# A sandwich layer whose FFN blocks compute the first matmul of two tiles by Strassen's scheme

## The chip, the cores and the metric

The kernel runs on one core of a Trainium2 chip. The metric is the device time of one execution in microseconds (us), lower is better. Engines are named as in the profile: PE (TensorE, matmuls), PEld (its weight loads), DVE (VectorE), ACT (ScalarE), POOL (GpSimd), SP (SyncE, which issues DMAs). Each engine runs its own instructions strictly in the order in which the program lists them; engines wait for each other only through semaphores.

## The reference, cut to what matters

2048 tokens of 256 features, in fp32: a gated linear attention with a layernorm on each side, and then six FFN blocks, again with a layernorm ahead and behind.

```
def _block(x, w1, b1, w2, b2):                     # HIDDEN = 1024, DIM = 256
    h = jax.nn.gelu(jnp.einsum('bsd,hd->bsh', x, w1) + b1, approximate=False)
    return jnp.einsum('bsh,dh->bsd', h, w2) + b2 + x
for i in range(6):
    x = _block(x, W1[i], B1[i], W2[i], B2[i])
    if i < 5:
        x = _layernorm(x, LN_G[i], LN_B[i])
```

The change touches the FFN blocks 1 to 4 alone. The attention, block 0 and block 5 compute what they did.

## The kernel before, in words

**Tiles.** The tokens are cut into four tiles of 512 (`TOK`). In the FFN, tile t of block b has the number n = 4b + t. Features lie on the partitions: a tile's input is two chunks (k = 0, 1) of 128 features by 512 tokens. Every fp32 operand X is kept as a rounded high part and a rest (`XH` and `XL` for the input, `WH` and `WL` for weights, `HH` and `HL` for the hidden layer), and a product is three matmuls, low by high, high by low, high by high, accumulated in fp32 in PSUM.

**One unit.** The hidden layer's 1024 features are eight slices j. For each (n, j), `mm1` (L326) makes 2 chunks x 3 = 6 matmuls of 512 columns into one of the four PSUM banks 0 to 3. ACT reads the bank twice, `ghi` (L970, gelu into `HH`) and `gf` (L979, gelu in place). DVE's `hlo` (L564) subtracts the two and writes `HL`. Then `mm2` (L340) makes 6 more matmuls into the tile's two accumulators (banks 4 to 7). `HH` and `HL` are rings of four slices. The PE list of blocks 1 to 5 is a loop over g = 8n + j (L400): `mm1` of unit g, then `mm2` of unit g - 3 (`LAG`).

**Between the blocks.** When the eighth `mm2` of a tile is done, DVE adds bias and residual (`y`, L572). Then comes a layernorm over features, that is over partitions, in many steps: `sum1` (POOL), `tr1`, `red1` (DVE), `put1` and `got1` (DMAs through DRAM, which spread the sums over the partitions), `tot1`, `mub`, `ctr` (DVE), `sqr` (ACT), `sum2` (POOL), `tr2`, `red2` (DVE), `put2`, `got2` (DMAs), `tot2`, `vae` (DVE), `rsd` (POOL, L1259, a power of -1/2), `rsb`, `nn` (DVE). At last `xhi` (ACT) and `xlo` (DVE) make the two parts of the next block's input, on which `mm1` of tile n + 4 waits. `got1` and `got2` (L1347 and L1359) are four transfers each, one for each 32 partitions.

**Weights.** A block's weights come in four pieces of 128x1024 (`ldp` on SP, into the two halves of `STG`); ACT's `wp_hi` and POOL's `wp_lo`, two halves of 512 each, split a piece.

**Order.** Every engine's list is written out by hand up to about tile 5 and for the last tiles; between them loops over n give each tile the same order on DVE, ACT, POOL and SP.

## Time and profile before

| | |
|---|---|
| median of 3 runs | 625.25 us (625.02 to 625.41) |
| the profiled execution's own time | 625.31 us |
| its span in the profile | 623.5 us (1.8 us lie around it) |
| PE busy | 617.3 us, 99% of the span, 2893 matmuls |
| DVE busy | 459.9 us, 74% |
| ACT busy | 409.0 us, 66% |
| POOL busy | 248.7 us, 40% |
| granted TensorE clock | 0.998 of full speed (2.4 GHz) |

Busy times of engines are not to be added, since they run side by side. A matmul's duration in the profile is the time from its start to its modelled end, and matmuls overlap; the distance between the starts of two is what one costs. An engine's idle time is put down to what released it.

### The profile page before, as it was taken

Reading aid. Unit: us, or ns where it says so; the run is one execution under the profiler, and the core shown is the slowest. Engines: PE = TensorE matmul, PEld = TensorE weight load, DVE = VectorE, ACT = ScalarE, POOL = GpSimd, SP = SyncE. Lnnn points to the kernel's source line nnn. Section 1 sums busy time; section 2 is a strip of 40 time slices with the busy share of each in tenths; the row PEclk is TensorE's granted clock in tenths of the full one; section 3 lists DMA queues with packets and bytes.
Section 4 is the critical chain, followed back from the end, with each engine's and each line's share of the span. In section 5 each row is a group of like instructions: output and inputs, shape, how many; then the busy total and the mean of one; then the engine's idle time right before and its main releaser. Section 6 shows DMA issues by size and latency. Waiting matters only on the chain.

```text
span 623.5 us, 8868 instructions
## 1 busy us (share of the span) xinstructions
PE 617.3 (99%) x2893; PEld 516.5 (83%) x2893; DVE 459.9 (74%) x826; ACT 409.0 (66%) x688; POOL 248.7 (40%) x233
## 2 busy tenths in 40 slices
PE   9999999999999999999999999999999999999996
PEld 7888888888888888888888888888888888888886
DVE  6999758886677778676787667767766867666676
ACT  6999986778756675566566556755656665555554
POOL 6666501537434353334532253442344422301234
PEclk9999999999999999999999999999999999999999
DMA  7210000003111020101200110200111100003544
GB/s 293 69 35 1 2 2 0 4 1 106 36 39 40 7 68 6 37 6 37 58 20 3 39 39 2 72 6 5 37 39 38 38 4 6 5 3 68 94 91 156
DMA packets 55821, 25.13 MB, mean 40 GB/s; under 512 B 46816, under 2 KB 51808, under 8 KB 55776
## 3 DMA queue, kind: packets, MB, share of 16 engines
q1 hardware_dynamic: 53376, 24.05, 15.2%
q10 hardware_dynamic: 2400, 0.52, 0.4%
q8 instruction: 23, 0.38, 0.3%
q14 instruction: 22, 0.18, 0.1%
HBM read 20.03 MB, written 4.52 MB: 39 GB/s over the span
## 4 chain that ended last, share of the span: by engine, by line
PE 95%; DVE 1%; DMA 1%; POOL 1%; ACT 0%; issue 0%; ACTq 0%; SPq 0%
PE BK L166 47%; PE BK L356 40%; PE BK L306 4%; PE BK L267 1%; PE BK L270 1%; PE BK L268 1%; PE BK L240 1%; PE BK L260 0%; PE BK L252 0%; PE BK L251 0%; DMA X<-in_x 0%; PE BK L230 0%; DVE R L709 0%; DMA turns<-TB 0%; DMA R<-turns 0%; DVE ST L675 0%
## 5 line engine op out<-in xcount | busy, mean ns | idle before, releaser
L976 ACT ACTIVATE HH<-BK,SM 128x512 fp32r<-128x512 f32 x192 | 132.1, 689 | 153.3 <-PE BK L166 148.3
L569 DVE TENSOR_TENSOR HL<-BK,HH 128x512 fp32r<-128x512 f32 x192 | 131.2, 685 | 84.0 <-ACT BK L982 82.0
L166 PE MATMUL BK<-XH,WL 128*128 128x512 f32 x416 | 162.4, 390 | 0.0
L166 PE MATMUL BK<-XL,WH 128*128 128x512 f32 x416 | 162.1, 390 | 0.0
L166 PE MATMUL BK<-XH,WH 128*128 128x512 f32 x416 | 162.0, 389 | 0.0
L356 PE MATMUL BK<-HH,WL 128*128 128x512 f32 x368 | 143.5, 390 | 0.0
L356 PE MATMUL BK<-HH,WH 128*128 128x512 f32 x368 | 143.2, 389 | 0.0
L356 PE MATMUL BK<-HL,WH 128*128 128x512 f32 x368 | 143.2, 389 | 0.0
L982 ACT ACTIVATE BK<-BK,SM 128x512 f32<-128x512 f32 x192 | 125.2, 655 | 0.0
L166 PEld LDWEIGHTS BK<-XH,WL 128*128 128x128 f32 x416 | 78.1, 188 | 16.6 <-DVE MS L551 0.3
L166 PEld LDWEIGHTS BK<-XH,WH 128*128 128x128 f32 x416 | 78.1, 188 | 16.3
L166 PEld LDWEIGHTS BK<-XL,WH 128*128 128x128 f32 x416 | 78.1, 188 | 15.8
L1263 POOL TENSOR_TENSOR RN<-VN,MH 128x16 f32<-128x16 f32 x20 | 58.7, 2935 | 62.4 <-DVE VN L628 62.4
L356 PEld LDWEIGHTS BK<-HL,WH 128*128 128x128 f32 x368 | 69.1, 188 | 14.3
L356 PEld LDWEIGHTS BK<-HH,WH 128*128 128x128 f32 x368 | 69.1, 188 | 14.3
L356 PEld LDWEIGHTS BK<-HH,WL 128*128 128x128 f32 x368 | 69.1, 188 | 14.2
L1177 POOL TENSOR_TENSOR WL<-STG,WH 128x512 fp32r<-128x512 f32 x48 | 64.5, 1361 | 36.7 <-ACT WH L850 36.6
L1257 POOL TENSOR_TENSOR SA<-SA,TB 128x512 f32<-128x512 f32 x20 | 25.9, 1293 | 127.3 <-ACT TB L991 127.3
L1253 POOL TENSOR_TENSOR SA<-R 128x512 f32<-128x512 f32 x20 | 25.9, 1293 | 39.6 <-DVE R L577 39.6
L1001 ACT ACTIVATE XH<-R,SM 128x512 fp32r<-128x512 f32 x40 | 27.7, 724 | 19.6 <-DVE R L642 19.6
L577 DVE SCALAR_TENSOR_TENSOR R<-BK,SM,R 128x512 f32<-128x512 f32 x46 | 33.5, 731 | 3.4 <-PE BK L356 3.4
L642 DVE SCALAR_TENSOR_TENSOR R<-R,SM,MB 128x512 f32<-128x512 f32 x40 | 35.5, 922 | 0.5
(165 smaller groups left out, 790.1 us busy)
## 6 DMA issues: line engine op xcount, KB each, us to landing
STG<-in_w SPq DMA_DIRECT2D x24, 512.0 KB, 3.8
G<-sums SPq DMA_DIRECT2D x160, 8.0 KB, 1.7
out<-R SPq DMA_DIRECT2D x16, 128.0 KB, 2.0
X<-in_x SPq DMA_DIRECT2D x3, 512.0 KB, 7.7
R<-turns SPq DMA_DIRECT2D x3, 512.0 KB, 4.1
turns<-SA SPq DMA_DIRECT2D x12, 64.0 KB, 2.0
sums<-P SPq DMA_DIRECT2D x40, 8.0 KB, 1.4
R<-in_wv SPq DMA_DIRECT2D x1, 512.0 KB, 5.4
```

Of the source, the lines that this page charges most:

```text
L166: r = eng.matmul(dst, s, m, start=i == 0, stop=i == len(todo) - 1)
L356: r = eng.matmul(acc_of(n)[k][:, :], w, h[:, hs, :], start=(j == 0 and i == 0), stop=(j == 7 and i == 2))
L569: eng.tensor_tensor(HL[:, g % HR, :], bank["mm1", n, j][:, :], HH[:, g % HR, :].bitcast(f32), ALU.subtract).then_inc(S["hlo"], 1)
L577: eng.scalar_tensor_tensor(feat(t, k), by_chunk(acc_of(n)[k][:, :]), BS[:, 2 * b + k:2 * b + k + 1], feat(t, k), ALU.add, ALU.add).then_in ...
L642: eng.scalar_tensor_tensor(feat(t, k), feat(t, k), LG[:, 2 * b + k:2 * b + k + 1], by_chunk(MB[:, 1, :]), ALU.mult, ALU.mult).then_inc(S[" ...
L976: eng.activation(HH[:, g % HR, :], bank["mm1", n, j][:, :], ACT.Gelu, bias=B1[:, 8 * (n // 4) + j:8 * (n // 4) + j + 1]).then_inc(S["ghi"], 1)
L982: eng.activation(ps[:, :], ps[:, :], ACT.Gelu, bias=B1[:, 8 * (n // 4) + j:8 * (n // 4) + j + 1]).then_inc(S["gf"], 1)
L1001: eng.activation(by_chunk(XH[:, F_SLOT[t], k, :]), feat(t, k), ACT.Identity, bias=LB[:, 2 * b + k:2 * b + k + 1]).then_inc(S["xhi"], 1)
L1177: eng.tensor_tensor(WL[:, b % 2, a:a + 512], STG[:, p % 2, 512 * h:512 * h + 512], WH[:, b % 2, a:a + 512].bitcast(f32), ALU.subtract).the ...
L1253: eng.tensor_tensor(by_chunk(SA[:, :]), feat(n % 4, 0), feat(n % 4, 1), ALU.add).then_inc(S["sum1"], 1)
L1257: eng.tensor_tensor(SA[:, :], SA[:, :], TB[:, :], ALU.add).then_inc(S["sum2"], 1)
L1263: eng.tensor_tensor(RN[:, :], VN[:, :], MH[:, :], ALU.pow).then_inc(S["rsd"], 1)
```

## The change

In blocks 1 to 4 the tiles 0 and 1 become a **pair**. Their first layer is a product of 2x2 blocks: the weights (two halves of the hidden features by two chunks, for each q of 0 to 3 the slices q and q + 4) and the input (two chunks by two tiles). Instead of eight block products of three matmuls each, seven are made, `prod1` to `prod7`, on sums of blocks:

- Sums of weights, `sadd` on POOL from `STG` into `SB` (four of 128x512 a pair), split by `shi` (ACT, two of 128x1024, into `UH` and `OH`, which the attention had used) and `slo` (POOL, four of 128x512, into `UL` and `OL`).
- Sums of inputs, `tsum` on DVE into `QB` (four a pair), split by `thi` (ACT) and `tlo` (DVE). Of the four plain inputs three are still needed and split, `bhi` (ACT) and `blo` (DVE).
- Products that go into more than one result are carried by copies: for each q ACT's `bcopy` copies bank a to bank c, and `tcopy` copies bank e to `KB`; DVE's `dsum` writes c + `KB` to bank d, and `esum` writes c + `KB` to bank e. PE goes on accumulating on a, c and d.

The four units of a q are numbered by `place`: (second tile, q), (first tile, q), (first, q + 4), (second, q + 4). Their `ghi`, `gf`, `hlo` and `mm2` stay what they were; in the PE list one `mm2` stands behind every two products. Behind the pair the last three `mm2` come right after the first `mm1` of tile 2.

Also: `put1` and `put2` write the sums to DRAM in another arrangement, from which `got1` and `got2` fetch them in **one** transfer of 128 rows of 256 bytes. All lists of blocks 1 to 4 (and the end of block 0's, from the place where DVE has its last `l2_mv`) are written out anew, for DVE, ACT, POOL and SP. PE's list up to the end of block 0 is what it was, and so are all lists of the last tiles.

```
+def place(n, j):
+    if not paired(n):
+        return 8 * n + j
+    return 32 * (n // 4) + 4 * (j % 4) + ((1, 2) if n % 4 == 0 else (0, 3))[j // 4]
...
+            def product(dst, s, m, first, last):
+                for i, (w, v) in enumerate(((s[1], m[0]), (s[0], m[1]), (s[0], m[0]))):
+                    r = eng.matmul(dst[:, :], w, v, start=first and i == 0, stop=last and i == 2, skip_group_check=True)
+                return r
+
+            def prod1(b, q, a, c, d, e):
+                claim(a)
+                pe.wait_ge(S["plo"], 7 * (b - 1) + 3)
+                pe.wait_ge(S["wp_lo"], 8 * b + 4)
+                bank["pair", b, q] = BK[a], BK[c], BK[d], BK[e]
+                bank["before", b, q] = freed[c], freed[d], freed[e]
+                for x, (n, j) in ((a, (4 * b + 1, q)), (d, (4 * b, q)), (e, (4 * b, q + 4)), (c, (4 * b + 1, q + 4))):
+                    bank["mm1", n, j] = BK[x]
+                    freed[x] = S["hlo"], place(n, j) + 1
+                product(BK[a], w_ffn(b, 128 * q, 128), home(B11), True, True).then_inc(S["prod"], 1)
+
+            def prod2(b, q):
+                pe.wait_ge(S["plo"], 7 * (b - 1) + 6)
+                pe.wait_ge(S["pcopy"], 8 * (b - 1) + 2 * q + 1)
+                product(bank["pair", b, q][0], w_ffn(b, 1024 + 128 * q, 128), home(B21), False, True).then_inc(S["mm1"], 1)
+
+            def prod3(b, q):
+                pe.wait_ge(S["plo"], 7 * (b - 1) + 1)
+                pe.wait_ge(S["slo"], 4 * b)
+                pe.wait_ge(S["padd"], 8 * (b - 1) + 2 * q + 1)
+                product(bank["pair", b, q][2], s_weights(3, q), home(B22), False, True).then_inc(S["mm1"], 1)
+
+            def prod4(b, q):
+                pe.wait_ge(S["plo"], 7 * b)
+                pe.wait_ge(S["padd"], 8 * (b - 1) + 2 * q + 2)
+                product(bank["pair", b, q][1], w_ffn(b, 1536 + 128 * q, 128), t_home(b, 3), False, True).then_inc(S["mm1"], 1)
+
+            def prod5(b, q):
+                before = bank["before", b, q][2]
+                pe.wait_ge(*before)
+                pe.wait_ge(S["plo"], 7 * (b - 1) + 4)
+                pe.wait_ge(S["slo"], 4 * b - 3)
+                product(bank["pair", b, q][3], s_weights(0, q), t_home(b, 1), True, True).then_inc(S["prod"], 1)
+
+            def prod6(b, q):
+                pe.wait_ge(S["plo"], 7 * (b - 1) + 5)
+                pe.wait_ge(S["slo"], 4 * b - 2)
+                pe.wait_ge(S["pcopy"], 8 * (b - 1) + 2 * q + 1)
+                product(bank["pair", b, q][1], s_weights(1, q), t_home(b, 2), False, True).then_inc(S["prod"], 1)
+
+            def prod7(b, q):
+                pe.wait_ge(S["plo"], 7 * (b - 1) + 2)
+                pe.wait_ge(S["slo"], 4 * b - 1)
+                pe.wait_ge(S["padd"], 8 * (b - 1) + 2 * q + 1)
+                product(bank["pair", b, q][1], s_weights(2, q), t_home(b, 0), False, True).then_inc(S["mm1"], 1)
...
-            for g in range(8 * 4, 8 * (4 * NB - 1)):
-                mm1(g // 8, g % 8, STEADY[g % 4])
-                mm2((g - LAG) // 8, (g - LAG) % 8)
+            for b in range(1, NB):
+                if b in PAIRED:
+                    a, e, c, d = STEADY
+                    for q in range(4):
+                        g = 32 * b + 4 * q
+                        mm2(*unit(g - 3))
+                        prod1(b, q, a, c, d, e)
+                        prod5(b, q)
+                        mm2(*unit(g - 2))
+                        prod2(b, q)
+                        prod6(b, q)
+                        mm2(*unit(g - 1))
+                        prod3(b, q)
+                        prod7(b, q)
+                        mm2(*unit(g))
+                        prod4(b, q)
+                        e, c, d = d, e, c
+                first_g = 32 * b + (16 if b in PAIRED else 0)
+                for g in range(first_g, min(32 * b + 32, 8 * (4 * NB - 1))):
+                    mm1(*unit(g), STEADY[g % 4])
+                    if b not in PAIRED or g > first_g + 2:
+                        mm2(*unit(g - LAG))
+                    elif g == first_g:
+                        for back in (3, 2, 1):
+                            mm2(*unit(g - back))
...
+            def tsum(b, i):
...
+                ve.wait_ge(S["nn"], 2 * n + (2, 3, 3, 4)[i])
+                if i > 1:
+                    ve.wait_ge(S["tsum"], 4 * (b - 1) + i)
+                dst, bias = by_chunk(QB[:, i, :]), LB[:, p + 1:p + 2]
+                if i == 0:
+                    ve.wait_ge(S["bias"], 2)
+                    r = eng.scalar_tensor_tensor(dst, feat(0, 1), DL[:, b - 1:b], feat(0, 0), ALU.add, ALU.subtract)
+                elif i == 1:
+                    r = eng.tensor_tensor(dst, feat(0, 0), feat(1, 0), ALU.subtract)
+                elif i == 2:
+                    r = eng.scalar_tensor_tensor(dst, feat(0, 1), bias, by_chunk(QB[:, 1, :]), ALU.add, ALU.subtract)
+                else:
+                    r = eng.scalar_tensor_tensor(dst, feat(1, 1), bias, by_chunk(QB[:, 2, :]), ALU.add, ALU.subtract)
+                r.then_inc(S["tsum"], 1)
+            def blo(b, i):
+                t, k = ((0, 1), (1, 0), (1, 1))[i]
+                hi, lo = b_home(i)
+                ve.wait_ge(S["phi"], 7 * (b - 1) + (1, 3, 6)[i])
+                eng.scalar_tensor_tensor(by_chunk(lo), feat(t, k), LB[:, 2 * (b - 1) + k:2 * (b - 1) + k + 1],
+                                         by_chunk(hi.bitcast(f32)), ALU.add, ALU.subtract).then_inc(S["plo"], 1)
+
+            def tlo(b, i):
+                hi, lo = t_home(b, i)
+                ve.wait_ge(S["phi"], 7 * (b - 1) + (2, 4, 5, 7)[i])
+                eng.tensor_tensor(lo, QB[:, i, :], hi.bitcast(f32), ALU.subtract).then_inc(S["plo"], 1)
+
+            def dsum(b, q):
+                _, c, d, _ = bank["pair", b, q]
+                ve.wait_ge(S["prod"], 12 * (b - 1) + 3 * q + 3)
+                ve.wait_ge(S["pcopy"], 8 * (b - 1) + 2 * q + 2)
+                ve.wait_ge(*bank["before", b, q][1])
+                eng.tensor_tensor(d[:, :], c[:, :], KB[:, q % 2, :], ALU.add).then_inc(S["padd"], 1)
+
+            def esum(b, q):
+                _, c, _, e = bank["pair", b, q]
+                ve.wait_ge(S["mm1"], place(4 * b, q + 4) + 1)
+                ve.wait_ge(S["pcopy"], 8 * (b - 1) + 2 * q + 2)
+                eng.tensor_tensor(e[:, :], c[:, :], KB[:, q % 2, :], ALU.add).then_inc(S["padd"], 1)
...
+
+            def bhi(b, i):
...
+                eng.activation(by_chunk(b_home(i)[0]), feat(t, k), ACT.Identity,
+                               bias=LB[:, 2 * (b - 1) + k:2 * (b - 1) + k + 1]).then_inc(S["phi"], 1)
+
+            def thi(b, i):
...
+                eng.activation(t_home(b, i)[0], QB[:, i, :], ACT.Copy).then_inc(S["phi"], 1)
+
+            def shi(b, h):
...
+                eng.activation((UH, OH)[h][:, :, :], SB[:, 2 * h:2 * h + 2, :], ACT.Copy).then_inc(S["shi"], 1)
+
+            def bcopy(b, q):
+                a, c, _, _ = bank["pair", b, q]
+                ac.wait_ge(S["prod"], 12 * (b - 1) + 3 * q + 1)
+                ac.wait_ge(*bank["before", b, q][0])
+                eng.activation(c[:, :], a[:, :], ACT.Copy).then_inc(S["pcopy"], 1)
+
+            def tcopy(b, q):
...
+                eng.activation(KB[:, q % 2, :], bank["pair", b, q][3][:, :], ACT.Copy).then_inc(S["pcopy"], 1)
+
+            def sadd(b, i):
...
+                a11, a21 = STG[:, 1, 0:512], STG[:, 1, 512:1024]
+                a12, a22 = STG[:, 0, 0:512], STG[:, 0, 512:1024]
+                if i in (1, 3):
+                    po.wait_ge(S["sadd"], 4 * (b - 1) + (1 if i == 1 else 2))
+                left, right, op = ((a21, a22, ALU.add), (SB[:, 0, :], a11, ALU.subtract), (a11, a21, ALU.subtract),
+                                   (a12, SB[:, 1, :], ALU.subtract))[i]
+                eng.tensor_tensor(SB[:, i, :], left, right, op).then_inc(S["sadd"], 1)
+
+            def slo(b, i):
+                hi, lo = (UH, OH)[i // 2], (UL, OL)[i // 2]
+                po.wait_ge(S["shi"], 2 * (b - 1) + i // 2 + 1)
+                eng.tensor_tensor(lo[:, i % 2, :], SB[:, i, :], hi[:, i % 2, :].bitcast(f32),
+                                  ALU.subtract).then_inc(S["slo"], 1)
...
             def ldp(p):
                 b, i = (p - 1) // 4, (p - 1) % 4
                 if p == 2:
-                    sp.wait_ge(S["wo_lo"], 1)
+                    sp.wait_ge(S["w_lo"], W_LO["o"])
                 elif p > 2:
                     sp.wait_ge(S["wp_lo"], 2 * (p - 2))
+                if b in PAIRED and i > 1:
+                    sp.wait_ge(S["sadd"], 4 * (b - 1) + i + 1)
                 src = (w1 if i < 2 else w2)[b][:, (i % 2) * 1024:(i % 2) * 1024 + 1024]
                 eng.dma_start(STG[:, p % 2, :], src).then_inc(S["ldp1"] if p % 2 else S["ldp0"], 16)
 
             def put1(n):
                 sp.wait_ge(S["red1"], n + 1)
-                eng.dma_start(SUMS[n, 0], P1[:, n % 2, :]).then_inc(S["put1"], 16)
+                eng.dma_start(SUMS[n, 0].rearrange("q (g b) -> g q b", g=4), P1[:, n % 2, :]).then_inc(S["put1"], 16)
 
             def got1(n):
                 sp.wait_ge(S["put1"], 16 * n + 16)
-                if n:
-                    sp.wait_ge(S["tot1"], n)
-                for h in range(4):
-                    eng.dma_start(G1[32 * h:32 * h + 32, n % 2],
-                                  SUMS[n, 0].rearrange("(g q) b -> q g b", g=4)).then_inc(S["got1"], 16)
+                if n > 1:
+                    sp.wait_ge(S["tot1"], n - 1)
+                eng.dma_start(G1[:, n % 2].rearrange("p g b -> p (g b)"),
+                              SUMS[n, 0].unsqueeze(0).to_broadcast([4, 32, 64])).then_inc(S[f"got1_{n % 2}"], 16)
```

**PE, block 2, first q of the pair.** Bank 2 is c, bank 0 is d, banks 4 to 7 accumulate `mm2`. The changed list, from `prod6` to `prod3`:

```order
L403 MATMUL BK2<-XH,UL 128x512
L403 MATMUL BK2<-XL,UH 128x512
L403 MATMUL BK2<-XH,UH 128x512
L471 MATMUL BK4<-HH,WL 128x512
L471 MATMUL BK4<-HH,WH 128x512
L471 MATMUL BK4<-HL,WH 128x512
L471 MATMUL BK5<-HH,WL 128x512
L471 MATMUL BK5<-HH,WH 128x512
L471 MATMUL BK5<-HL,WH 128x512
L403 MATMUL BK0<-XH,OL 128x512
L403 MATMUL BK0<-XL,OH 128x512
L403 MATMUL BK0<-XH,OH 128x512
```

The same place in the list before, from the second half of `mm1` (8, 2) over `mm2` (7, 7):

```order
L166 MATMUL BK1<-XH,WL 128x512
L166 MATMUL BK1<-XL,WH 128x512
L166 MATMUL BK1<-XH,WH 128x512
L356 MATMUL BK4<-HH,WL 128x512
L356 MATMUL BK4<-HH,WH 128x512
L356 MATMUL BK4<-HL,WH 128x512
L356 MATMUL BK5<-HH,WL 128x512
L356 MATMUL BK5<-HH,WH 128x512
L356 MATMUL BK5<-HL,WH 128x512
L166 MATMUL BK2<-XH,WL 128x512
L166 MATMUL BK2<-XL,WH 128x512
L166 MATMUL BK2<-XH,WH 128x512
```

Six matmuls of one `mm1` became two products of three on different banks, one of which (on bank 0) waits for DVE's `dsum`, and only one `mm2` of six lies ahead of it.

**DVE, the same pair, from the second `esum` to the third `dsum`.** L830 is `dsum`, L836 `esum`, L706 `hlo`; the others are steps of the layernorms of tiles 6 and 7:

```order
L836 TENSOR_TENSOR BK0<-BK1,KB 128x512
L721 STREAM_TRANSPOSE TB<-SA 128x512
L706 TENSOR_TENSOR HL<-BK2,HH 128x512
L725 TENSOR_REDUCE P1<-TB 128x16
L706 TENSOR_TENSOR HL<-BK0,HH 128x512
L759 TENSOR_REDUCE VS<-G2 128x16
L765 TENSOR_SCALAR VN<-VS 128x16
L706 TENSOR_TENSOR HL<-BK1,HH 128x512
L731 TENSOR_REDUCE MU<-G1 128x16
L771 STREAM_TRANSPOSE MB<-RN 128x512
L737 STREAM_TRANSPOSE MB<-MU 128x512
L830 TENSOR_TENSOR BK1<-BK0,KB 128x512
```

A piece of the list before, between the same kinds of steps (L569 is `hlo`, L577 `y`):

```order
L569 TENSOR_TENSOR HL<-BK1,HH 128x512
L569 TENSOR_TENSOR HL<-BK2,HH 128x512
L612 STREAM_TRANSPOSE TB<-SA 128x512
L577 SCALAR_TENSOR_TENSOR R<-BK6,SM,R 128x4x128
L616 TENSOR_REDUCE P2<-TB 128x16
L577 SCALAR_TENSOR_TENSOR R<-BK7,SM,R 128x4x128
L569 TENSOR_TENSOR HL<-BK0,HH 128x512
L584 STREAM_TRANSPOSE TB<-SA 128x512
L588 TENSOR_REDUCE P1<-TB 128x16
L569 TENSOR_TENSOR HL<-BK3,HH 128x512
```

Two additions on which PE waits now stand in the row, between the steps of two layernorms, where before `hlo` and one tile's layernorm (with the next tile's first steps) alternated.

**DVE, ahead of the same pair**, the stretch in which its inputs are made (L804 to L810 `tsum`, L817 `blo`, L823 `tlo`, L771 `rsb`, L779 `nn`, L721 `tr1`):

```order
L817 SCALAR_TENSOR_TENSOR XL<-R,SM,XH 128x512
L779 SCALAR_TENSOR_TENSOR R<-R,SM,MB 128x4x128
L706 TENSOR_TENSOR HL<-BK1,HH 128x512
L806 TENSOR_TENSOR QB<-R 128x512
L779 SCALAR_TENSOR_TENSOR R<-R,SM,MB 128x4x128
L808 SCALAR_TENSOR_TENSOR QB<-R,SM,QB 128x512
L706 TENSOR_TENSOR HL<-BK2,HH 128x512
L810 SCALAR_TENSOR_TENSOR QB<-R,SM,QB 128x512
L823 TENSOR_TENSOR XL<-QB,XH 128x512
L817 SCALAR_TENSOR_TENSOR XL<-R,SM,XH 128x512
L823 TENSOR_TENSOR XL<-QB,XH 128x512 x2
L817 SCALAR_TENSOR_TENSOR XL<-R,SM,XH 128x512
```

Before, the end of tile 5's layernorm stood at this place, between `hlo` of (7, 5) and the tile's end (L634 is `rsb`, L642 `nn`, L648 `xlo`, L594 `tot1`):

```order
L569 TENSOR_TENSOR HL<-BK1,HH 128x512
L569 TENSOR_TENSOR HL<-BK2,HH 128x512
L634 STREAM_TRANSPOSE MB<-RN 128x512
L642 SCALAR_TENSOR_TENSOR R<-R,SM,MB 128x4x128 x2
L569 TENSOR_TENSOR HL<-BK0,HH 128x512
L648 SCALAR_TENSOR_TENSOR XL<-R,SM,XH 128x512 x2
L594 TENSOR_REDUCE MU<-G1 128x16
```

Before, two `nn` and two `xlo` stood in each tile's stretch. Now 13 instructions that make the pair's inputs (two `nn`, four `tsum`, three `blo`, four `tlo`) stand in the last four units ahead of the pair, between `hlo` of (7, 3) and of (7, 7).

## Rows read from the trace of the kernel before

**Rows 1.** Page: span, busy time and count of each engine, chain by engine and line:

```profile
span 623.5 us, 8868 instructions
PE 617.3 (99%) x2893; PEld 516.5 (83%) x2893; DVE 459.9 (74%) x826; ACT 409.0 (66%) x688; POOL 248.7 (40%) x233
PE 95%; DVE 1%; DMA 1%; POOL 1%; ACT 0%; issue 0%; ACTq 0%; SPq 0%
```

**Rows 2.** A stretch as long as a block: us, PE, PEld, DVE, ACT, POOL busy (count), clock:

```profile
300.04:387.08 87.04, 87.04 (x385) 72.10 (x385) 63.40 (x101) 53.11 (x85) 32.99 (x20) 1.00 0.12 29
```

**Rows 3.** Timeline, one unit: start, duration (us), engine, line; idle and releaser bracketed:

```profile
302.13 0.39 PE L166 MATMUL BK<-XH,WH 128*128 128x512 f32 x1
302.13 0.19 PEld L356 LDWEIGHTS BK<-HH,WL 128*128 128x128 f32 x1
302.36 0.39 PE L356 MATMUL BK<-HH,WL 128*128 128x512 f32 x1
302.56 0.69 ACT L976 ACTIVATE HH<-BK,SM 128x512 fp32r<-128x512 f32 x1 [1.48 <-PE BK L166]
303.14 0.66 ACT L982 ACTIVATE BK<-BK,SM 128x512 f32<-128x512 f32 x1
305.86 0.66 ACT L982 ACTIVATE BK<-BK,SM 128x512 f32<-128x512 f32 x1
306.55 0.69 DVE L569 TENSOR_TENSOR HL<-BK,HH 128x512 fp32r<-128x512 f32 x1 [0.63 <-ACT BK L982]
```

**Rows 4.** Groups by line and form: busy us, mean ns; idle before, releaser:

```profile
L976 ACT ACTIVATE HH<-BK,SM 128x512 fp32r<-128x512 f32 x192 | 132.1, 689 | 153.3 <-PE BK L166 148.3 <-PE BK L356 3.4 <-PE BK L371 1.0
L569 DVE TENSOR_TENSOR HL<-BK,HH 128x512 fp32r<-128x512 f32 x192 | 131.2, 685 | 84.0 <-ACT BK L982 82.0 <-PE BK L356 1.5 <-issue 0.3
L521 DVE SCALAR_TENSOR_TENSOR BK<-KB,BK 128x512 f32<-128x512 f32 x8 | 5.5, 691 | 2.0 <-ACT KB L942 1.3 <-PE BK L166 0.7
L961 ACT ACTIVATE OH<-QB 128x512 fp32r<-128x512 f32 x16 | 10.1, 628 | 0.7 <-DVE QB L533 0.7
L850 ACT ACTIVATE WH<-STG 128x1024 fp32r<-128x1024 f32 x24 | 25.5, 1061 | 4.2 <-DMA STG<-in_w 2.5 <-PE BK L356 1.7
L1177 POOL TENSOR_TENSOR WL<-STG,WH 128x512 fp32r<-128x512 f32 x48 | 64.5, 1361 | 36.7 <-ACT WH L850 36.6
L1253 POOL TENSOR_TENSOR SA<-R 128x512 f32<-128x512 f32 x20 | 25.9, 1293 | 39.6 <-DVE R L577 39.6
```

**Rows 5.** Timeline of DVE and POOL where both read SBUF, and beside a power:

```profile
375.57 2.98 POOL L1177 TENSOR_TENSOR WL<-STG,WH 128x512 fp32r<-128x512 f32 x2 [4.03 <-ACT WH L850]
376.14 2.97 DVE L648 SCALAR_TENSOR_TENSOR XL<-R,SM,XH 128x512 fp32r<-128x512 f32 x2 [0.90 <-ACT XH L1001]
396.68 1.78 DVE L642 SCALAR_TENSOR_TENSOR R<-R,SM,MB 128x512 f32<-128x512 f32 x1
398.98 1.40 DVE L648 SCALAR_TENSOR_TENSOR XL<-R,SM,XH 128x512 fp32r<-128x512 f32 x2
195.14 3.35 POOL L1263 TENSOR_TENSOR RN<-VN,MH 128x16 f32<-128x16 f32 x1 [3.19 <-DVE VN L628]
196.63 0.74 DVE L648 SCALAR_TENSOR_TENSOR XL<-R,SM,XH 128x512 fp32r<-128x512 f32 x1
L1263 POOL TENSOR_TENSOR RN<-VN,MH 128x16 f32<-128x16 f32 x20 | 58.7, 2935 | 62.4 <-DVE VN L628 62.4
```

**Rows 6.** Timeline of SP's queue; then transfers with KB and us to landing:

```profile
363.51 0.34 SPq L1357 DMA_DIRECT2D sums<-P  x1
364.93 1.74 SPq L1364 DMA_DIRECT2D G<-sums  x4
turns<-SA SPq DMA_DIRECT2D x12, 64.0 KB, 2.0
sums<-P SPq DMA_DIRECT2D x40, 8.0 KB, 1.4
```

**Rows 7.** Waits: who waited for whom: us in total, times, longest:

```profile
DVE MU L594 <- DMA G<-sums: 5.8, 4, 2.8
```

534 lines of the change are left out of this document (339 added, 195 removed).

## The prediction

> **What bounds the kernel now.** I read the page's busy times and its chain first: PE is busy 617.3 of 623.5 us, and 95% of the chain that ended last is PE's [rows 1]. Then a stretch as long as one block: in 87.04 us PE has no gap, at the full granted clock, while DVE is busy 63.4, ACT 53.1 and POOL 33.0 us [rows 2]. A block is 32 units of 12 matmuls, so 87.04 / 384 = 0.227 us a matmul, which is also the distance of two starts (302.13, 302.36) [rows 3]; I call 3 matmuls a product (0.68 us) and one half of a unit 1.36 us. Only fewer matmuls, or gaps, can move the time. Next comes how far the helpers lag. From the slot after an `mm1` (302.36) ACT starts 0.20 later, its second gelu 0.58 behind the first, that one runs 0.66, and `hlo` follows after 0.03 and takes 0.69 [rows 3]: 2.15 us in all. The weights of a matmul load one slot (0.23) ahead of it [rows 3], so a wait is free only if it is over 0.23 us before the slot. In the old list six halves (8.16 us) lie between an `mm1` and its `mm2`: 5.8 us are to spare, and the idle times of DVE and ACT (82.0 us of `hlo` waiting for ACT, 148.3 of ACT waiting for PE) show that margin from the other side [rows 4].
>
> **What is removed.** A pair had 16 units' first layers, 96 matmuls; now 4 x 7 products of 3 are 84. Twelve fewer in each of four blocks are 48 x 0.227 = 10.9 us, all of it on the path. No cheaper form replaces them and none dearer: all are 512 columns with weights of 128x128. The profiled execution took 625.3 (span and 1.8 us around it), 0.06 above the median of the runs. So the floor is 625.3 - 10.9 = 614.4 us. A block then has 84.3 us.
>
> **What is added, per block.** DVE: eight `dsum`/`esum`, a PSUM and an SBUF input and a PSUM output; the nearest row is `kv`, 0.69 [rows 4], 5.5 us. Four `tsum` and four `tlo` less one `xlo`: two SBUF inputs, 0.70 to 0.75 undisturbed (two of them in a row take 1.40 [rows 5]), 5.1 us. DVE goes from 63.4 to 74.0 of 84.3. ACT: eight copies at 0.63 to 0.66 (5.0 to 5.3), four `thi` at 0.63, two `shi` at 1.06 [rows 4], less an `xhi`: about 9 us, 53 to 62 of 84. POOL: eight of 1.29 to 1.36 [rows 4], 10.6, so 33 to 44. None of the three is full. What counts is whether each thing is there in its slot.
>
> **Price of the port.** Where POOL's `wp_lo` overlaps DVE instructions with two SBUF inputs, two of these take 2.97 instead of 1.40 us, and one 1.78 instead of about 0.72; POOL's two take 2.98 where two of 1.29 would be 2.6 [rows 4, 5]. So a collision costs DVE 0.75 to 1.1 us. POOL's such work goes from 16 to 24 a block and DVE's from 24 to 31. Where the new list puts them side by side is uncertain; I charge about 2 us more DVE time a block, 76 of 84.3 (90%). The Trainium skill ("SBUF — State Buffer", Who interferes with whom) says the same of the kind of instruction: DVE with two SBUF inputs contends with a GpSimd instruction that reads SBUF, and the loser blocks for the whole of the other's. `dsum`, `esum` and `hlo` read one input from PSUM and would be spared by it.
>
> **The margins inside a pair.** One q takes 7 x 0.68 + 4 x 1.36 = 10.2 us. With `prod1` at 0: `prod5` 0.68, `mm2` 1.36, `prod2` 2.72, `prod6` 3.40, `mm2` 4.08, `prod3` 5.44, `prod7` 6.12, `mm2` 6.80, `prod4` 8.16, the next q's first `mm2` 8.84. Then:
> - `bcopy` after `prod1`: 0.68 + 0.20 + 0.66 = 1.54, wanted 2.49. Hidden.
> - `dsum` after `prod6`: 4.08 + 0.20 + 0.69 = 4.97 (4.28 is its earliest start), wanted for `prod3` at 5.21. Margin 0.2.
> - `esum` after `prod7`: 6.80 + 0.89 = 7.69, wanted for `prod4` at 7.93. Margin 0.2.
> - the unit ended by `prod2`: 3.40 + 2.15 = 5.55, wanted 6.57. Margin 1.0.
> - the unit ended by `prod3`: its gelu ends 7.56, but its `hlo` stands behind `esum`, so 7.0 + 0.61 + 0.69 = 8.3, wanted at 8.61. Margin 0.3, if nothing is between. In 6 of the 16 q's one instruction of about 0.62 us is between `esum` and this `hlo` (twice in blocks 2 and 4, once in 1 and 3); then 8.92, late by 0.3. **6 x 0.3 = 1.8 us.**
> - DVE has 2.7 us from `dsum` to `esum`. `hlo` cannot start before the gelu's end at 4.83 and leaves at 5.5; two steps of 0.62 more bring it to 6.8 or 7.0. In the third q of blocks 2, 3 and 4 one or two of these have two SBUF inputs; one collision of 0.75 makes `esum` 0.5 late. I take it in half of them: **0.7 us.**
> - From `esum` to the next `dsum` DVE has 7.5 us for 5 to 6.3 us of work, but the steps wait for DMAs and POOL. The transfer's change is on this path: before, `put` at 363.51 let the four `got` start at 364.93; they take 1.74 to issue, one every 0.43 [rows 6]. One transfer instead is there 1.3 us sooner. The new arrangement for `put` I bound by its own 1.4 and the 2.0 of the scattered `turns` [rows 6]. For the third q of block 2 I get `mub` done about 0.1 us ahead of the moment when `dsum` could start. Nothing charged, up to 0.5 us a q in the range.
>
> **The start of a pair.** `prod1` needs three of the seven input parts. From the slot after `mm1` (7, 3) to `prod1` are 13.6 us. DVE can start 1.5 us in (the first `hlo`) and has four `hlo`, four `tsum`, `tr1`, `rsb`, two `blo`, two `nn` and one `tlo` to do: 15 instructions at some 0.65 (two overlap by a little, so that a pair takes 1.40), 9.7 us. 13.6 - 1.5 - 9.7 - 0.2 = 2.2 us would be to spare. But this stretch begins late, behind the two layernorms of the pair before. In block 1, `sum1` of tile 4 stands on POOL behind four `slo` (to 8.0 us after the pair's last product), and adding the steps as they are listed (the two round trips of 3.3 us each, two `rsd` of 2.9 [rows 5] one behind the other on POOL) I get the second `nn` of tile 4 done, and that `hlo` started, 35.2 us after the last product instead of at 32.8: 2.4 us late. With it the 2.2 to spare are gone and one more part comes after ACT's split: `prod1` some 0.4 late. The other parts then come in time for `prod5` and `prod2`. **4 x 0.4 = 1.6 us**; between 0 and 2 us each for the range. Block 1's pair is prepared beside the last attention steps; I charge it no more.
>
> **The sum.** 614.4 + 1.8 + 0.7 + 1.6 = **618.5 us**. The tail's lists are unchanged, so it follows PE as before. SP's list gets shorter (two issues a tile layernorm in place of eight for `got`), `ldp` stands ahead of no late `got` by my walk; cover gone, each would cost 0.5 or so, in the range.
>
> **Rivals.**
> 1. All hand-overs fit, 614.4 to 615.6: the arithmetic alone. For it: nothing on DVE, ACT or POOL is full [rows 2]. Against it: 32 hand-overs with a margin of 0.2 us. About 615.
> 2. DVE's lateness shows at most hand-overs, 0.25 us at 32 places, beside the 1.8 and 1.6: 614.4 + 8.0 + 3.4 = 625.8 at worst, with half of it 622. For it: DVE at 90% with in-order waits, where the trace shows waits for `got` of up to 2.8 us at single places that were harmless so far [rows 7].
> 3. **Slower**: DVE instructions blocked by POOL's new `sadd` and `slo` reach `dsum` and `esum`. A hit costs 1.1 us less the 0.2 of margin. From (10.9 - 3.4) / 0.9 = 8 hits on (of 32) nothing is left of the gain; with 16 it is 614.4 + 3.4 + 14.4 = 632. Against it: the POOL list keeps the eight apart from the middle of the pair, mostly at its end and behind it, where PE has 5.8 us of margin.
> 4. **`rsd` as the blocker**: in blocks 2, 3 and 4 the pair's second `rsd` runs just beside `nn` of its first tile. If a power of 2.9 us held DVE for its whole length, three pairs would start 2.9 late: 618.5 + 8.7 = 627.2. The one place in the trace where this can be seen speaks against it: `xlo` at 196.63 took 0.74 us inside the power of 195.14 to 198.49, which itself took 3.35 instead of 2.91 [rows 5]. By the rule of the same page of the Trainium skill, a lock that is held for the full instruction, DVE would have waited there until 198.49; the row doesn't show it, and I go by the row.
> 5. The change doesn't do what it says: the lists hold exactly 48 matmuls fewer and nothing else added on PE, so only 0.02 for it.
>
> **How the numbers follow.** Forecast (616 to 620.5) 0.50; rival 1 0.22; rival 2 0.17, a quarter of it within or above 624; rival 3 0.06; rival 4 0.03; no effect 0.02. The range to hold 8 in 10 runs from 614.4 to 623.0: it takes in rival 1 and the milder part of rival 2, and leaves out some 0.13 above. A measurement of this kernel can tell about 0.2% (1.2 us) from no change, so faster means under 624.0: 0.50 + 0.22 + 0.15 = 0.87. Within: 0.04. Slower: 0.09.
>
> **What would show it right or wrong.** PE's count must fall by 48 to 2845, its starts keep 0.227 us. In each paired block gaps of 0.2 to 0.5 us ahead of the products that wait for DVE (L403), and ahead of an `mm2` waiting for `hlo`, should sum to some 1 us, and DVE should be busy 74 to 76 us of a block. Gaps ahead of `prod1` of more than 2 us, or `nn` of 2.9 us or more beside `rsd`, would make rival 4; many `tsum`, `tlo`, `nn` of 1.5 us and more beside POOL, with gaps right behind them, rival 3. `got` should land as one transfer in 1.5 to 2.0 us. The forecast fails above all if the chain of the pair's two layernorms comes later than my walk: every us there is a us at each of four pair starts.

## The result, and the profile after

The changed kernel takes 630.62 us (median of 6 runs, 628.75 to 636.45) against 625.23 (6 runs, 625.02 to 625.41) for the kernel before: a ratio of 1.0099, 95% interval 1.0073 to 1.0124. It is **slower by 5.4 us**, or 1%, where 618.5 was forecast, and its runs lie 8 us apart, those of the kernel before 0.4. The profiled execution took 628.75, 1.8 us more than its span.

The page of the changed kernel: span, busy time and count of each engine, and the chain that ended last by engine and by line (to be read against [rows 1]):

```profile
span 626.9 us, 8837 instructions
PE 614.4 (98%) x2845; PEld 505.5 (81%) x2845; DVE 505.1 (81%) x886; ACT 438.3 (70%) x740; POOL 297.9 (48%) x266
PE 59%; DVE 18%; DMA 8%; issue 7%; ACT 5%; POOL 3%; SPq 0%; DVEq 0%; ACTq 0%; POOLq 0%
PE BK L471 22%; PE BK L228 22%; PE BK L403 7%; DMA sums<-P 3%; DMA G<-sums 3%; DVE HL L706 3%; PE BK L368 2%; DVE R L779 2%; PE BK L486 2%; DVE R L714 1%; POOL WL L1479 1%; DVE XL L817 1%; POOL SA L1587 1%; ACT BK L1195 1%; DMA STG<-in_w 1%
```

The 48 matmuls are gone (2893 to 2845), and PE still looks full at 98%. The chain tells more than the share: before it was PE for 95%, now for 59%. It runs through DVE (18%), and through the two transfers of the layernorm sums, `sums<-P` and `G<-sums`, for 3% each.

The four blocks with a pair, one row each: busy us (count) of PE, PEld, DVE, ACT and POOL, the granted clock, DMA share and GB/s (compare [rows 2]):

```profile
186.00:270.00 84.00, 82.34 (x357) 66.81 (x358) 72.65 (x113) 59.15 (x95) 47.64 (x30) 1.00 0.10 29
270.00:354.50 84.50, 82.79 (x359) 66.81 (x358) 69.68 (x111) 57.65 (x93) 44.34 (x28) 1.00 0.10 30
354.50:439.00 84.50, 83.55 (x360) 66.81 (x359) 69.20 (x111) 57.46 (x93) 39.30 (x24) 1.00 0.10 29
439.00:523.00 84.00, 83.74 (x365) 67.89 (x364) 68.40 (x112) 57.74 (x95) 29.99 (x19) 1.00 0.06 17
```

No helper is full: DVE has 68 to 73 us of 84, less than the 74 to 76 that I had added up. What is late is late at single places. I took the distance of PE's starts less 0.227 us a matmul as the loss, and call a single place where it is over 0.03 us a **stop**. The loss sums to 1.95 us at the end of block 0 and 4.1, 3.3, 3.2 and 1.4 us in the four blocks, 13.95 in all; 628.75 less the floor of 614.4 is 14.35.

Waits in the changed kernel, who waited for whom: us in total, times, longest (compare [rows 7]):

```profile
DVE MU L731 <- DMA G<-sums: 14.0, 8, 4.2
DVE VS L759 <- DMA G<-sums: 9.0, 11, 2.7
PE BK L403 <- DVE BK L830: 3.4, 5, 1.4
PEld BK L471 <- DVE HL L706: 3.6, 9, 0.6
```

`tot1` (L731) waits 14.0 us for its sums instead of 5.8, once for 4.2. PE waits for `dsum` (L830) at five places and for `hlo` (L706) in small pieces. Two long stops show the two causes I found at single places.

**Block 2, q 2.** Timeline of SP's queue, then DVE, then PE:

```profile
290.49 0.46 SPq L1670 DMA_DIRECT2D STG<-in_w  x1
291.61 0.55 SPq L1674 DMA_DIRECT2D sums<-P  x1
292.31 0.37 SPq L1670 DMA_DIRECT2D STG<-in_w  x1
294.37 0.53 SPq L1680 DMA_DIRECT2D G<-sums  x1
297.50 0.26 DVE L731 TENSOR_REDUCE MU<-G 128x16 f32<-128x64 f32 x1 [4.23 <-DMA G<-sums]
297.67 0.70 DVE L771 STREAM_TRANSPOSE MB<-RN 128x512 f32<-128x512 f32 x1
298.30 0.67 DVE L737 STREAM_TRANSPOSE MB<-MU 128x512 f32<-128x512 f32 x1
298.89 0.67 DVE L830 TENSOR_TENSOR BK<-BK,KB 128x512 f32<-128x512 f32 x1
299.61 0.50 PE L403 MATMUL BK<-XH,OL 128*128 128x512 f32 x1 [1.39 <-DVE BK L830]
299.95 0.40 PE L403 MATMUL BK<-XL,OH 128*128 128x512 f32 x1
```

`put` is issued between two weight pieces of 512 KB, `got` can go 2.76 us later, and DVE reads the sums 3.13 us after that. At a place of the same trace where no piece was issued between them the first distance was 1.94 (287.95 to 289.89; 1.42 in [rows 6]) and the second 2.3 (289.89 to 292.19). `dsum` stands behind `tot1`, `rsb` and `mub` in DVE's list, so `prod3` starts 1.55 us late. The second matmul then comes 0.34 after the first instead of 0.23: most stops cost another 0.11 us in this way, about 20 times here, 2 us in all.

**The start of pair 1.** Timeline of DVE (`tlo`, `blo`), of POOL (`sadd`), and of PE (`prod2`):

```profile
183.57 1.26 DVE L823 TENSOR_TENSOR XL<-QB,XH 128x512 fp32r<-128x512 f32 x1
184.75 1.76 DVE L817 SCALAR_TENSOR_TENSOR XL<-R,SM,XH 128x512 fp32r<-128x512 f32 x1
182.98 1.30 POOL L1502 TENSOR_TENSOR SB<-STG 128x512 f32<-128x512 f32 x1 [3.67 <-issue]
184.36 1.61 POOL L1502 TENSOR_TENSOR SB<-SB,STG 128x512 f32<-128x512 f32 x1
185.93 1.73 POOL L1502 TENSOR_TENSOR SB<-STG 128x512 f32<-128x512 f32 x1
186.57 0.50 PE L403 MATMUL BK<-XH,WL 128*128 128x512 f32 x1 [1.11 <-DVE XL L817]
```

Beside POOL's `sadd`, `tlo` takes 1.26 instead of 0.68 us and `blo` 1.76 instead of 0.74, and `prod2` is 1.27 us late.

**The end of block 0.** PE's transposes of the last attention tile, in the changed kernel and then in the first experiment below, in which `sadd` and `slo` are cut to 32 columns:

```profile
155.52 0.66 PE L302 MATMUL BK<-ID,R 128*128 128x128 f32 x4 [1.53 <-DVE HL L706]
155.07 0.66 PE L302 MATMUL BK<-ID,R 128*128 128x128 f32 x4 [0.96 <-DVE HL L706]
```

Of the 1.95 us lost here this is 1.53. Without `sadd` beside DVE 0.96 remains, and in a repair below (block 2's `sadd` later, and block 1's), where `sadd` starts only after these two `nn` and they take 0.75 and 0.74 us, PE still stops for 1.12. So no more than half of the 1.95 us is `sadd`. The rest fits DVE's new list, which has `rsb`, `nn`, `tot1`, `nn` and `mub` ahead of that `hlo`; no run took that apart.

### The profile page after: what moved, and what is told of

It reads as the page before. It is cut to its first block, busy times and chain, and to the rows that moved or that the text cites. A ratio compares the mean times of both kernels' runs of the same rounds, so it can differ in the third digit from the quotient of the medians.

```text
span 626.9 us, 8837 instructions
## 1 busy us (share of the span) xinstructions
PE 614.4 (98%) x2845; PEld 505.5 (81%) x2845; DVE 505.1 (81%) x886; ACT 438.3 (70%) x740; POOL 297.9 (48%) x266
## 4 chain that ended last, share of the span: by engine, by line
PE 59%; DVE 18%; DMA 8%; issue 7%; ACT 5%; POOL 3%; SPq 0%; DVEq 0%; ACTq 0%; POOLq 0%
PE BK L471 22%; PE BK L228 22%; PE BK L403 7%; DMA sums<-P 3%; DMA G<-sums 3%; DVE HL L706 3%; PE BK L368 2%; DVE R L779 2%; PE BK L486 2%; DVE R L714 1%; POOL WL L1479 1%; DVE XL L817 1%; POOL SA L1587 1%; ACT BK L1195 1%; DMA STG<-in_w 1%
## 5 line engine op out<-in xcount | busy, mean ns | idle before, releaser
L706 DVE TENSOR_TENSOR HL<-BK,HH 128x512 fp32r<-128x512 f32 x192 | 129.6, 679 | 42.0 <-ACT BK L1195 41.5
L471 PE MATMUL BK<-HH,WL 128*128 128x512 f32 x368 | 145.0, 394 | 0.4 <-DVE HL L706 0.3
L228 PE MATMUL BK<-XH,WL 128*128 128x512 f32 x288 | 112.7, 391 | 0.0
L228 PE MATMUL BK<-XH,WH 128*128 128x512 f32 x288 | 112.2, 390 | 0.0
L228 PE MATMUL BK<-XL,WH 128*128 128x512 f32 x288 | 112.2, 390 | 0.0
L228 PEld LDWEIGHTS BK<-XH,WL 128*128 128x128 f32 x288 | 54.1, 188 | 11.9 <-DVE XL L637 0.3
L228 PEld LDWEIGHTS BK<-XH,WH 128*128 128x128 f32 x288 | 54.0, 188 | 11.4
L228 PEld LDWEIGHTS BK<-XL,WH 128*128 128x128 f32 x288 | 54.1, 188 | 10.7
L779 DVE SCALAR_TENSOR_TENSOR R<-R,SM,MB 128x512 f32<-128x512 f32 x40 | 38.2, 977 | 0.1
L1583 POOL TENSOR_TENSOR SA<-R 128x512 f32<-128x512 f32 x20 | 26.8, 1340 | 16.2 <-DVE R L714 15.5
L744 DVE SCALAR_TENSOR_TENSOR R<-MB,R 128x512 f32<-128x512 f32 x40 | 34.0, 867 | 0.3
```

Source lines behind the costliest of these rows:

```text
L228: r = eng.matmul(dst, s, m, start=i == 0, stop=i == len(todo) - 1)
L471: r = eng.matmul(acc_of(n)[k][:, :], w, h[:, hs, :], start=(j == 0 and i == 0), stop=(j == 7 and i == 2))
L706: eng.tensor_tensor(HL[:, g % HR, :], bank["mm1", n, j][:, :], HH[:, g % HR, :].bitcast(f32), ALU.subtract).then_inc(S["hlo"], 1)
L744: eng.scalar_tensor_tensor(feat(t, k), by_chunk(MB[:, 0, :]), -1.0 / 256, feat(t, k), ALU.mult, ALU.add).then_inc(S["ctr"], 1)
L779: eng.scalar_tensor_tensor(feat(t, k), feat(t, k), LG[:, 2 * b + k:2 * b + k + 1], by_chunk(MB[:, 1, :]), ALU.mult, ALU.mult).then_inc(S[" ...
```

## Experiments

Theories: **P**, POOL's `sadd` and `slo` hold up DVE instructions with two SBUF inputs; **T**, the transfers of the sums come late behind weight pieces, and DVE waits for them in front of `dsum`; **M**, `dsum`, `esum` and `hlo` have so little room that any lateness of DVE becomes a stop.

**One suspected cause taken away at a time.** Here 625.22 is the kernel before beside them.

```diff
-eng.tensor_tensor(SB[:, i, :], left, right, op)
+eng.tensor_tensor(SB[:, i, 0:32], left[:, 0:32], right[:, 0:32], op)
...                                                   # and slo in the same way
```

> The changed kernel with the sums of weights (sadd) and their rests (slo) cut to the first 32 of 512 columns: POOL keeps its list and signals, but the 32 new instructions that read SBUF are nearly gone; the weight sums are left out in the other columns. Theory P (the port: POOL's new instructions hold up DVE's with two SBUF inputs, and these come late to PE): 4 us or more of the 14.5 us of gaps go, the 1.95 us at the end of block 0 among them, so 626 or below. Theory T (the round trips of the layernorm sums through DRAM are what comes late): under 1 us, the 4.2 us wait for the sums ahead of the third dsum of block 2 stays, some 630. Theory M (the hand-overs dsum and esum have no margin, whatever makes DVE late): 1 to 3 us.

Measured 626.86 us (625.85 to 631.87, 7 runs; ratio 1.0035, 1.0011 to 1.0059): 3.8 less than the change. The stops ahead of the products on plain weights (`W` in the rows; `U` and `O` are the sums) fall from 2.0 to 0.9 us, those for `dsum` stay (4.5 in 7 stops; 4.3 in 7 in the changed kernel). P is a part, not the whole.

```diff
-eng.dma_start(STG[:, p % 2, :], src)
+eng.dma_start(STG[:, p % 2, 0:32], src[:, 0:32])      # for p > 8
```

> The changed kernel with the weight pieces from the ninth on (blocks 2 to 5) loaded with 32 of their 1024 columns, so that 16 transfers of 512 KB become 16 KB; the rest of the weights is stale. Theory T: the small transfers of the sums no longer queue behind the weights, the put and got of a layernorm take 1.9 and 2.2 us at each place instead of up to 2.8 and 3.1, the 4.2 us wait in block 2 goes with its gap of 1.7 us and the spread between runs shrinks; about 627 to 628. Theories P and M: no change beyond 0.5 us, about 630.

Measured 628.76 us (628.13 to 630.2, 4 runs; ratio 1.0057, 1.0042 to 1.0073): 1.9 less, but the two intervals (1.0073 to 1.0124 for the change) touch, so the size is uncertain. The trace is clearer. SP's queue and DVE at block 2, q 2:

```profile
293.01 0.55 SPq L1677 DMA_DIRECT2D sums<-P  x1
294.97 0.53 SPq L1683 DMA_DIRECT2D G<-sums  x1
297.22 0.27 DVE L731 TENSOR_REDUCE MU<-G 128x16 f32<-128x64 f32 x1 [2.41 <-DMA G<-sums]
```

The two distances of 2.76 and 3.13 us are 1.96 and 2.25 here, and the stop of 1.55 us is gone. The stops for `dsum` fall from 4.3 in 7 to 1.4 in 5 (longest 0.63), the longest wait of L731 from 4.2 to 2.4. But at the start of the first pair one stop of 2.3 us, for `tlo`, stands in place of the 1.27, and the granted clock is at half for some 3 us behind it. T is a part too.

The transfer by itself: the old one (four `got`) put into the changed kernel, and the new one put into the kernel before.

```diff
-eng.dma_start(G1[:, n % 2].rearrange("p g b -> p (g b)"),
-              SUMS[n, 0].unsqueeze(0).to_broadcast([4, 32, 64]))
+for h in range(4):
+    eng.dma_start(G1[32 * h:32 * h + 32, n % 2],
+                  SUMS[n, 0].rearrange("(g q) b -> q g b", g=4))
...                                                   # got2 too, and put1, put2 with the rows in order
```

> The changed kernel with the sums written and fetched as before: put with rows in order, four got. If the new put costs its 0.5 us (1.94 against 1.42 us to the following got) and the one got saves 1.3 us, this is slower than the changed kernel, 631 to 634. If the one transfer lands no sooner than the last of four did, it is faster by the put's 0.5 us at each of 8 round trips on the critical places, 627 to 629.

> The kernel before with the new put and the one got alone. Its margins of 5.8 us hide either form: all theories say 625.2 within 0.5 us. The trace prices the form itself: from put to got 1.9 us where it was 1.42, and DVE's wait for the sums (14.6 us in total before) says which form lands sooner.

Measured 638.18 us (637.87 to 640.85, 4 runs; ratio 1.0214, 1.0193 to 1.0235) and 625.27 us (625.14 to 625.49, 10 runs; ratio 1.0001, 0.9991 to 1.001). In the kernel before the new form is worth nothing: DVE's waits for sums fall from 14.6 to 7.2 us and the time stays, so they were harmless. In the changed kernel it saves 7.5 us. Waits of the changed kernel with the old transfer, as above:

```profile
DVE MU L731 <- DMA G<-sums: 19.7, 10, 4.9
DVE VS L759 <- DMA G<-sums: 17.4, 18, 3.2
```

So the same transfer has no price in one kernel and a high one in the other, as M says. Not all of the 7.5 us is waiting: behind a stop of 2.33 us at 213.56 the profiled run has 3 us with a granted clock of 0.50 (215 to 218 us), where the changed kernel has 1.00.

**More room for the hand-overs.** In the first, PE takes each q as `prod1 prod5 mm2 prod6 prod2 mm2 prod7 prod3 mm2 prod4 mm2`, and from q 1 on every `mm2` at its place is that of one unit further back, so that one `mm2` fewer lies ahead of each product of q 1 to 3; in the second, `dsum` and `esum` are short; in the third, `dsum` stands ahead of the waits in DVE's list; in the fourth, both the first and the third.

```diff
 prod1(b, q, a, c, d, e)
 prod5(b, q)
 mm2(*unit(g - 2 if q == 0 else g - 3))
-prod2(b, q)
 prod6(b, q)
+prod2(b, q)
...                                                   # prod7 and prod3, the other mm2, and the waits of esum and ghi
```

> The changed kernel with the same 84 + 96 matmuls a pair in another order on TensorE: q is now prod1, prod5, mm2, prod6, prod2, mm2, prod7, prod3, mm2, prod4 (mm2), so that dsum's input ends one product earlier and esum's too. Worked out from the starts, the room between the end of dsum or esum and its product grows from 0.2 to about 0.9 us. DVE, ACT and POOL lists are those of the changed kernel. Theory M (the hand-overs of dsum, esum and hlo have 0.2 to 0.3 us of room, whatever makes DVE late): of the 14.5 us of gaps the dsum part (4.3 in 7) loses up to 0.7 each, the hlo and esum part (1.5 to 2) goes, with 0.11 us of restart per gap: 5 us less, about 625. Theory T (DVE waits up to 4.2 us for the layernorm sums in front of dsum): only the two long gaps of 1.55 and 0.98 shrink to 0.9 and 0.3, the short ones go all the same, about 626. Theory P (the gap is POOL's sadd and slo against DVE): most lost time is at the pair starts and stays, 628 to 629.

```diff
-eng.tensor_tensor(d[:, :], c[:, :], KB[:, q % 2, :], ALU.add)
+eng.tensor_tensor(d[:, 0:32], c[:, 0:32], KB[:, q % 2, 0:32], ALU.add)
...                                                   # and esum in the same way
```

> The changed kernel, but dsum and esum add 32 of the 512 columns (the other columns of those first-layer sums are left out). Each ends about 0.5 us sooner; lists and orders as they are. DVE has 16 us less to do over the four pairs. Theory M: room of 0.2 becomes 0.7 us, gaps for dsum 4.3 -> about 1.5 us and for hlo 1.2 -> 0: about 626. Theory P or T: the long gaps (1.27, 1.55, 0.98) lose at most 0.5 each: 628.

```diff
-tot1(7); rsb(6); mub(7); dsum(2, 2); hlo(9, 2); ctr(7, 0)
-ctr(7, 1); esum(2, 2); hlo(8, 2)
+dsum(2, 2); hlo(9, 2); tot1(7); rsb(6); mub(7)
+esum(2, 2); ctr(7, 0); ctr(7, 1); hlo(8, 2)
...                                                   # one of six places
```

> The changed kernel with six places of VectorE's list changed, nothing else: dsum stands ahead of tot1, mub, rsb, ctr and nn instead of behind them (pairs 1 to 4), so that no wait for the layernorm's sums and no ctr or nn stands in front of it. Theory T (waits for the sums' transfer, 4.2 and 2.4 us at two places, and ctr or nn at three): the gaps of 1.55, 0.98, 0.64 and 0.59 ahead of prod3 go, 3.8 us with their restarts: about 626.5, and the wait of L731 for G in the list stays but behind dsum. Theory M or P: something else then comes late in the same stretch, 629 to 630.

> Both of the edits before: TensorE's order with 0.9 us of room and VectorE's list with dsum first. T and M together: left are the gaps at the start of the pairs (block 0's end 1.95, prod2 at 186.57 1.27, others small), 4 us of gaps over the floor of 614.4: 619 to 621. P: 1 to 2 us below the better of the two, not under 625.

Beside the kernel before at 625.2 us:

| kernel | us (runs) | ratio, 95% interval | stops for dsum / hlo, us in all |
|---|---|---|---|
| PE's order | 635.28 (4) | 1.0161 (1.0148 to 1.0174) | 9.4 / 0.3 |
| short dsum, esum | 627.3 (9) | 1.0036 (1.0024 to 1.0048) | 2.0 / 1.3 |
| DVE's list | 631.48 (4) | 1.01 (1.0087 to 1.0113) | 0.3 / 5.9 |
| order and list | 634.39 (4) | 1.0146 (1.0131 to 1.016) | 5.1 / 0.8 |

Shorter instructions help by 3.3 us, as M says. The first and the last missed what every theory expected of them. Of the third M and P had said that something else would then come late (629 to 630), which it did, at a somewhat higher price. In the kernel with DVE's list changed, DVE and then PE in the same q of block 2:

```profile
297.73 0.70 DVE L830 TENSOR_TENSOR BK<-BK,KB 128x512 f32<-128x512 f32 x1 [3.44 <-PE BK L403]
298.93 0.26 DVE L731 TENSOR_REDUCE MU<-G 128x16 f32<-128x64 f32 x1
301.12 1.28 DVE L744 SCALAR_TENSOR_TENSOR R<-MB,R 128x512 f32<-128x512 f32 x2
302.32 0.68 DVE L706 TENSOR_TENSOR HL<-BK,HH 128x512 fp32r<-128x512 f32 x1
303.06 0.50 PE L471 MATMUL BK<-HH,WL 128*128 128x512 f32 x1 [0.54 <-DVE HL L706]
```

`dsum` now waits for PE, not for the DMA, and the 1.55 us are gone. But `ctr` twice (1.28) stands in front of `hlo`, and a stop of 0.70 opens there; at the other places likewise: the stops for `dsum` fall from 4.3 to 0.3 us, and those for `hlo` grow from 1.2 to 5.9. In the kernel with PE's order changed, PE and DVE in block 3, q 1:

```profile
375.26 0.50 PE L403 MATMUL BK<-XH,UL 128*128 128x512 f32 x1 [1.07 <-ACT BK L1265]
377.94 0.27 DVE L762 TENSOR_REDUCE VS<-G 128x16 f32<-128x64 f32 x1 [2.81 <-DMA G<-sums]
378.35 0.70 DVE L833 TENSOR_TENSOR BK<-BK,KB 128x512 f32<-128x512 f32 x1
379.10 0.50 PE L403 MATMUL BK<-XH,OL 128*128 128x512 f32 x1 [0.80 <-DVE BK L833]
```

Counted from the pair's first `prod1`, the landing of the sums in front of `dsum` (`tot2`, L762) has not moved: 15.9 us in the changed kernel, 16.0 here. But PE, with one `mm2` fewer ahead of it, wants `dsum` after 16.2 us instead of 17.0, and so a wait that ended in time ends 0.8 us late. The order has a second fault, the line of 375.26: PE stops for ACT's `bcopy` (L1265), 3.1 us at four places here and 3.6 at seven in the fourth kernel; in the changed kernel it never does. In this q `bcopy` waits for an `hlo` (0.71 us, until 374.62), since the units that `prod2` and `prod3` end come a product later. So this run doesn't test M alone. Room worked out from PE's starts alone was not the room.

**All three taken away together, and repairs that keep all work.** The second moves `sadd` of blocks 1 and 2 off the collisions with two waits, the third is a gentler list (hlo straight behind esum), the fourth both.

> The changed kernel with three things left out at once that were left out singly: sadd and slo work on 32 columns (left out alone: 3.8 us less), weight pieces from the ninth on load 32 of 1024 columns (1.9 less), dsum and esum add 32 columns (3.3 less). If the three causes are separate and complete, 630.6 - 9.0 = 621.6. If they overlap (a gap needs two of them at once), each single one already took the shared part: 622.5 to 625. Under 617 it would say that nothing else costs anything beside the floor of 614.4.

```diff
+if b == 1:
+    po.wait_ge(S["nn"], 2)
+if b == 2:
+    po.wait_ge(S["plo"], 6)
...                                                   # and sum2(1) ahead of wp_lo(5, 1)
```

> The changed kernel with two waits added and one instruction moved on GpSimd, all work kept: the four sadd of block 1 start after the second nn of tile 0, those of block 2 after the pair's sixth small part (plo 6), and sum2(1) stands ahead of wp_lo(5,1). Theory P (the first two gaps are GpSimd's sadd beside DVE instructions with two SBUF inputs): the 1.95 us before block 1 and the 1.27 us at prod2 of its pair go, 3.2 us and two restarts: about 627. Rival (DVE is late there by its own list, or GpSimd's delay only moves the meeting to ctr or to wp_lo): at most 1 us less, 629.5 to 630.6.

> The changed kernel with five places of VectorE's list changed and one of ScalarE's: dsum ahead of tot1, mub, rsb and ctr as in the lists tried before, but hlo of the unit that prod3 ends straight behind esum, ahead of ctr and nn. Theory T (late sums in front of dsum are the loss, the lists before only put ctr in front of hlo instead): the dsum gaps of 1.55, 0.98, 0.64 and 0.59 go and no hlo gap comes: 626.5. Rival (the stretch is full: what is taken from in front of dsum is missing from the room of hlo or of the next dsum): 629 to 631.

> Both edits together, all work kept. If the causes are separate the gains add: 3.4 and 4 us, about 623, under the kernel before. If the same stretches were only waiting for something else in turn, 626 to 628.

Measured, beside 625.43 us for the kernel before: all three left out 619.95 us (618.79 to 620.53, 4 runs; ratio 0.9909, 0.9893 to 0.9926); the repairs 632.69 (4 runs; 1.0116, 1.0101 to 1.0131), 636.85 (4; 1.0181, 1.0163 to 1.02) and 638.72 (4; 1.0208, 1.0193 to 1.0223). The three together give 10.7 us, singly 3.8, 1.9 and 3.3, so they add within what runs that lie several us apart can tell. All three repairs came out slower than either theory had said. PE in the kernel with all three left out, from 186 to 523:

```profile
186.00:523.00 337.00, 336.65 (x1471) 275.33 (x1470) 265.10 (x451) 234.50 (x381) 139.42 (x100) 1.00 0.03 5
```

PE is busy 336.65 of 337.00 us, where it was 332.43 in the changed kernel. Of the 5.2 us that are left over the floor in its profiled run, some 3 are stops from 154 us on, 0.98 of them still at the end of block 0. Most of the rest lies in distances that are no stops: between 187 and 523 us the starts that are late by less than 0.03 us sum to 1.9 us (2.3 in the changed kernel, -0.2 in the kernel before). What makes those slots longer I did not find.

In the first repair ScalarE's `shi(1,0)` waited for the delayed `sadd` with the split of block 0's last input behind it, and PE stopped for 2.5 us at 163.00. The gentler list opened a stop of 2.9 us in block 3, ahead of `prod3`. Three single repairs followed, and the changed kernel again, all beside 625.13 us for the kernel before:

> The changed kernel with one wait added: the four sadd of block 2 start on GpSimd after six of the pair's small parts (plo) are there, instead of when the weight piece has landed. All work kept. Theory P: tlo and blo ahead of prod2 take 0.68 and 0.74 us instead of 1.26 and 1.76, the gaps of 1.27 and 0.42 us and their restarts go, nothing else moves: 1.7 to 2 us less, 628.7 (of 630.6). Rival (DVE is late there anyway): same as the changed kernel within 0.5 us.

> As the one before, and the four sadd of block 1 wait for the second nn of tile 0, with shi(1,0) moved behind sqr(1,1) in ScalarE's list, so that ScalarE's next pieces don't stand behind it, and sum2(1) ahead of wp_lo(5,1) on GpSimd. Theory P: the stop of 1.53 us at turn3 in block 0 shrinks by what the two nn lost (1.3 us) and the 1.95 us of block 0's end go to about 0.6: 627.4. Rival: the delayed sadd meet ctr of tile 1 and slo meets block 1's first sums; then no gain over the run before, or a loss of up to 1 us.

> As the one before, and in VectorE's list of block 2 dsum and hlo of q 2 stand ahead of tot1(7), rsb(6), mub(7), and hlo behind esum ahead of the two ctr. Theory T: the 1.55 us gap ahead of prod3 in that q goes; in the run that had this among five edits, 0.56 us for a ScalarE copy and 0.25 us for hlo came after it. So 0.8 to 1.7 us less than the run before: 626. Rival (full stretch): no gain.

> The changed kernel itself. Theory: its runs differ because stops longer than some length let TensorE's granted clock fall to one half for a few us (as seen in two experiments after stops of 2.4 and 2.8 us), and the stops hang on DMA landings that differ from run to run. Then a median near 630.6 with a spread of several us again, and in a profile over 630 us some stretch with a granted clock of 0.5, in one near 628.8 none. Rival: the spread has another source; then a slow profile shows more or longer gaps at full clock.

| kernel | us (range, runs) | ratio, 95% interval |
|---|---|---|
| block 2's sadd later | 630.57 (629.49 to 632.24, 5) | 1.0088 (1.0075 to 1.0101) |
| and block 1's | 632.8 (630.59 to 633.31, 4) | 1.011 (1.0096 to 1.0125) |
| and block 2's list | 632.2 (631.93 to 633.05, 4) | 1.0115 (1.0102 to 1.0128) |
| the change itself | 631.14 (629.36 to 633.63, 6) | 1.0098 (1.0082 to 1.0114) |

With block 2's `sadd` later, timeline of DVE, POOL and PE at the start of pair 1, and DVE and PE in its q 2:

```profile
183.50 0.68 DVE L823 TENSOR_TENSOR XL<-QB,XH 128x512 fp32r<-128x512 f32 x1
184.10 0.74 DVE L817 SCALAR_TENSOR_TENSOR XL<-R,SM,XH 128x512 fp32r<-128x512 f32 x1
185.07 1.29 POOL L1504 TENSOR_TENSOR SB<-STG 128x512 f32<-128x512 f32 x1 [5.83 <-DVE XL L817]
185.41 0.47 PE L403 MATMUL BK<-XH,WL 128*128 128x512 f32 x1
210.53 0.26 DVE L731 TENSOR_REDUCE MU<-G 128x16 f32<-128x64 f32 x1 [3.30 <-DMA G<-sums]
212.93 0.50 PE L403 MATMUL BK<-XH,OL 128*128 128x512 f32 x1 [1.91 <-DVE BK L830]
```

P is shown at its place: without `sadd` beside them the same two take 0.68 and 0.74, and the stop ahead of `prod2` falls from 1.27 to 0.19 us. But the 1.1 us gained there are gone before q 2: four small stops (for `hlo`, `dsum` and `esum`, with the matmul behind each) take 1.4 us where the changed kernel lost 0.3, and PE would reach `prod3` of q 2 at 210.85, in the changed kernel at 210.95. There the sums then land later: `got` is issued at 206.98 (206.92 in the changed kernel) and `tot1` starts at 210.53 instead of 209.54, so that PE stops 2.08 instead of 0.99 us. How much of that last delay is chance is open, for a second profile of the changed kernel, below, had 1.52 us at this place. In the second, `sum1` of tile 2 comes late on POOL (175.57 instead of 172.63), and PE stops 1.87 us for an `hlo` at 179.58; I did not follow that chain to its end. No version that keeps all work beat the kernel before.

**The clock.** The second profile of the changed kernel (631.91 us) differs from the first where block 0 ends. Its windows: length, PE, PEld, DVE, ACT and POOL busy, then the granted clock; and PE's timeline:

```profile
153.00:155.00 2.00, 0.97 (x6) 0.42 (x4) 2.00 (x4) 2.00 (x5) 2.00 (x2) 1.00 0.00 0
155.00:157.00 2.00, 0.71 (x4) 0.72 (x5) 2.00 (x5) 1.75 (x3) 2.00 (x2) 0.74 0.00 0
157.00:158.00 1.00, 1.00 (x4) 0.86 (x3) 1.00 (x2) 1.00 (x3) 1.00 (x2) 0.50 0.00 0
159.00:160.00 1.00, 1.00 (x5) 0.81 (x4) 1.00 (x2) 0.41 (x2) 1.00 (x2) 0.82 0.00 0
...
156.28 1.11 PE L302 MATMUL BK<-ID,R 128*128 128x128 f32 x4 [1.84 <-DVE HL L706]
158.05 0.63 PE L228 MATMUL BK<-XH,WH 128*128 128x512 f32 x1
158.48 0.63 PE L228 MATMUL BK<-XH,WL 128*128 128x512 f32 x1
```

After stops of 0.47 and 1.84 us the granted clock falls to 0.50 (1.2 of 2.4 GHz) for about 3 us, and a matmul there comes every 0.43 instead of 0.23 us. In the first profile the stop at this place was 1.53 us and the clock stayed at 1.00. The six matmuls there take 1.2 us more than at the full clock. The Trainium skill (TensorE: Matmul & The Clock Gate, What's actually happening) says that the throttled clock is the default and that activity releases it; the trace agrees in so far as the clock fell behind stops and came back behind some 3 us of matmuls. So much the same stop costs its length alone in one run, and half-clock matmuls besides in another. Nor does a stop's length alone decide: with the old transfer one of 2.33 us at 213.56 had the half clock behind it and one of 2.59 at 305.16 did not, and neither did the 2.08 us above. The mean granted clocks of the changed kernel's twelve runs say how much of the spread this is: the seven with 0.998 or more took 628.75 to 630.68 us, the five with 0.993 to 0.997 took 631.6 to 636.45. So all that lies above 631 us comes with a lower clock; the other 2 us I did not separate.

## Why the prediction was wrong

- **Removed work**: right. 48 matmuls fewer, 0.227 us each, the floor of 614.4 stands. Over it 4.1 us were forecast, and 14.35 came in the fastest run, the one profiled.
- **"From `esum` to the next `dsum` ... Nothing charged"**: the term that failed most. The stops ahead of `prod3` were 0.98 and 1.55 us behind late sums, 0.64 behind two `ctr` and 0.59 behind two `nn` of 3.15 together (beside `wp_lo` and `sum2`), 3.8 us in four q's. My bound for `put` (1.4 to 2.0 us) held undisturbed (1.94). What the walk lacked is that `put` and `got` take longer with the pieces issued around them: 2.76 and 3.13 us, and 1.96 and 2.25 with small pieces. I had looked at `ldp` only as a matter of issue order.
- **"I charge it no more"** for block 1's pair beside the last attention steps, and **"the POOL list keeps the eight apart"** in rival 3: the `sadd` of blocks 1 and 2 met `nn`, `tlo` and `blo` there. It cost 1.27 us at `prod2` and up to half of the 1.95 us at the end of block 0; the rest fits DVE's own list there, which I had not walked either. The price of a collision was right (0.6 to 1.0 us against 0.75 to 1.1), its places were not; I had looked at the middle of the pair and not at its start.
- **The start of a pair**, 4 x 0.4 = 1.6: the mechanism I feared, late layernorms of the pair before, is not to be seen. Pairs 2, 3 and 4 start without a stop over 0.1 us, pair 1 is late by the collision above.
- **The margins inside a pair**: 1.8 for `hlo` was right in kind. The six stops come in the blocks that I had named (one, two, one, two), but sum to 1.0 us, with one of 0.3 ahead of the first pair. 0.7 for `esum` measured 0.8 in 3 stops, and that is luck: I had put them in the third q, by collisions, and they are in the first and second, two of them behind a `tot1` that waits 0.46 and 0.40 us for its sums.
- **No term for the stop itself**: 0.11 us each, some 2 us in all; nor for the slots between the stops, 2.3 us late in all; nor for the clock, which comes on top in some runs.
- **The single transfer**: right in sign, 7.5 us in this kernel; but it was counted as a thing that was merely sooner.
- **Rivals**: 4, a block of 2.9 us, did not occur: the first `nn` of pairs 2, 3 and 4 (260.30, 348.48, 435.90 us) took 0.74, 0.74 and 0.73 us inside the power. 2 and 3 named the mechanisms but priced each alone; together, and with T, they gave more than the whole gain. Slower had 0.09. For rival 1 stood that no engine is full, which is true and decided nothing.
- **The range** was too narrow since the cases were taken as alternatives. The runs show causes that add: 3.8, 1.9 (uncertain) and 3.3 us singly, 10.7 together.

## What to carry to other kernels

When helpers must hand over twice within each 10 us on in-order lists, walk every place with its waits for DMAs in real time, not by busy shares: room counted from PE's own starts is none if DVE stands before a landing that doesn't move. Price small transfers with the large ones that are in flight beside them. What a repair gains at one place can be lost at the next ones, so test repairs on the whole kernel before believing a local gain, and count each stop with its restart.

## What I had not expected of the hardware

- A power of 16 columns on GpSimd (2.9 to 3.4 us) didn't hold up DVE's instructions with two SBUF inputs (0.74 us inside it), while `sadd`'s 512 columns cost them 0.6 to 1.0 us each.
- A small transfer beside 512 KB ones: `put` to `got` 1.94 us undisturbed, 2.76 beside them; `got` to use 2.3 and 3.1. With pieces of 16 KB in their place, 1.96 and 2.25.
- The matmul behind the first one after a wait comes 0.11 us late (0.34 instead of 0.23).
- A stop of 1.84 us shortly behind one of 0.47 came with half the clock for about 3 us; one of 1.53 at the same place did not. Stops of 2.3 us in two other profiles had it too, one of 2.59 and one of 2.08 did not.
